# A gated cross-attention block with eight experts on one core: the first expert's tokens are taken unweighted and its sum weighted apart, and the router's exponential moves to GpSimd

## The reference

```python
router_logits = x @ gate_w.T                      # 448 x 8
probs = softmax(router_logits)
topw, sel = top_k(probs, 2)
topw = topw / sum(topw)
combine = sum(one_hot(sel, 8) * topw[..., None], axis=1)
gate, up = split(x @ gate_up_w[e].T)              # 512 columns each, for every expert e
hact = up * gelu(gate)
expert_out = hact @ down_w[e].T
out = sum_e expert_out[e] * combine[:, e]
```

## Time and profile before

| | us |
|---|---|
| median of 3 runs | 279.33 (279.15 to 280.34) |
| the profiled execution | 282.56 |
| its span, first to last instruction | 280.8 |
| PE busy | 268.3 (96%) |
| DVE busy | 217.1 (77%) |
| ACT busy | 178.9 (64%) |
| POOL busy | 125.7 (45%) |

### The profile page before, as it was taken

The page is one execution under the profiler, slowest core; times in us unless marked ns, Lnnn a source line. Parts: engine busy times, 40 slices in busy tenths (PEclk is TensorE's granted clock), DMA queues, the critical chain, the costliest instruction groups (busy, mean ns, idle before and its releaser), DMA issues.

```text
span 280.8 us, 8075 instructions
## 1 busy us (share of the span) xinstructions
PE 268.3 (96%) x2807; PEld 220.5 (79%) x2807; DVE 217.1 (77%) x460; ACT 178.9 (64%) x369; POOL 125.7 (45%) x148
## 2 busy tenths in 40 slices
PE   7989899999999999999999999988989999999994
PEld 3466678888888888887988887876888788989962
DVE  4679778878887889788878897886566988888771
ACT  2546677677776777678668765564718877776500
POOL 3588852574466456455456210123520855554200
PEclk9999999999999999999999999997999999999999
DMA  7389972991992992794595399200000000000001
GB/s 249 100 203 206 192 188 57 244 234 39 234 234 71 247 223 79 179 239 133 156 234 159 79 219 292 80 0 2 2 2 1 0 4 0 0 1 0 0 0 33
DMA packets 10821, 32.40 MB, mean 115 GB/s; under 512 B 2688, under 2 KB 3200, under 8 KB 10784
## 3 DMA queue, kind: packets, MB, share of 16 engines
q1 hardware_dynamic: 10368, 31.80, 44.7%
q10 hardware_dynamic: 432, 0.33, 0.4%
HBM read 13.26 MB, written 0.23 MB: 48 GB/s over the span
## 4 chain that ended last, share of the span: by engine, by line
PE 79%; ACT 6%; DVE 6%; DMA 3%; issue 2%; POOL 1%; SPq 1%; DVEq 0%; ACTq 0%
PE max_ps L1065 15%; PE o_ps L1086 14%; PE score_ps L1045 14%; PE misc_ps L1024 8%; PE misc_ps L1017 4%; DMA kx<-k_high 3%; PE score_ps L1281 3%; ACT probs L560 3%; PE score_ps L1282 2%; PE score_ps L1283 2%; PE o_ps L1383 2%; PE misc_ps L1125 2%; DVE part_max L746 2%; PE o_ps L1281 2%; PE score_ps L1009 2%
## 5 line engine op out<-in xcount | busy, mean ns | idle before, releaser
L746 DVE TENSOR_REDUCE part_max<-max_ps 112x1 f32<-112x512 f32 (+1 forms) x192 | 117.6, 666 | 28.1 <-PE max_ps L1065 26.4
L560 ACT ACTIVATE probs<-score_ps 128x448 f32<-128x448 f32 x188 | 88.2, 548 | 13.8 <-PE score_ps L1045 13.5
L1065 PE MATMUL max_ps<-kx,qx 96*112 96x512 f32 (+1 forms) x192 | 79.7, 421 | 3.4 <-DMA kx<-k_high 1.5
L1045 PEld LDWEIGHTS score_ps<-qx,kx 104*128 104x128 f32 x376 | 64.4, 190 | 8.1 <-issue 0.7
L1045 PE MATMUL score_ps<-qx,kx 104*128 104x224 f32 x376 | 67.8, 278 | 0.0
L1086 PE MATMUL o_ps<-probs,v_sb 128*32 128x112 f32 (+1 forms) x1536 | 46.2, 265 | 1.1 <-ACT probs L560 0.6
L1086 PEld LDWEIGHTS o_ps<-probs,v_sb 128*32 128x32 f32 (+1 forms) x1536 | 38.4, 111 | 7.5 <-ACT probs L560 6.1
L1065 PEld LDWEIGHTS max_ps<-kx,qx 96*112 96x112 f32 x192 | 33.6, 176 | 9.9 <-issue 4.6
L554 ACT ACTIVATE v_sb<-misc_ps 128x512 f32<-128x512 f32 x24 | 14.4, 602 | 29.4 <-PE misc_ps L1024 29.4
L381 POOL TENSOR_TENSOR k_low<-k_full,k_high 128x512 fp32r<-128x512 f32 (+1 forms) x21 | 26.3, 1256 | 13.7 <-ACT k_full L542 13.4
L417 POOL CAST ctx_parts<-ctx_sb 128x512 fp32r<-128x512 f32 (+1 forms) x18 | 10.8, 602 | 41.5 <-PE misc_ps L1017 26.7
(11 more groups left out here) (192 smaller groups left out, 387.4 us busy)
## 6 DMA issues: line engine op xcount, KB each, us to landing
kx<-k_high SPq DMA_DIRECT2D x60, 187.5 KB, 4.6
kx<-k_low SPq DMA_DIRECT2D x30, 187.5 KB, 4.5
gu_sb<-in_guT SPq DMA_DIRECT2D x8, 512.0 KB, 5.2
ctx_sb<-in_ctxT SPq DMA_DIRECT2D x6, 494.0 KB, 5.5
ctx_sb<-in_ctxT SPq DMA_DIRECT2D x8, 256.0 KB, 2.8
dn_sb<-in_dnT SPq DMA_DIRECT2D x8, 256.0 KB, 5.7
ctx_sb<-in_ctxT SPq DMA_DIRECT2D x1, 750.0 KB, 6.3
kx<-k_high SPq DMA_DIRECT2D x4, 123.5 KB, 2.3
```

The source lines that it names most:

```text
L560: nc.scalar.activation(probs[:, (KT * h + t) % 8, :], bank[:, 0:SC // 2], ACT.Exp, scale=SCALE).then_inc(exp_done, 1)
L746: nc.vector.reduce_max(part_max[:, p, c:c + 1], max_ps[0:PC, bank, 0:size], AX.X).then_inc(max_taken, turns)
L1045: last = nc.tensor.matmul(bank[0:m, GC * g:GC * g + GC], kx[0:KR, 2 * par + h, g, 128 * t:128 * t + m], qx[0:KR, par, 2 * h + g, :], start ...
L1065: nc.tensor.matmul(max_ps[0:PC, bank, 0:size], qx[0:MR, par, 2 * h + p // 2, PC * (p % 2):PC * (p % 2) + PC], kx[0:MR, slot, p // 2, start ...
```

## The change

- **First expert.** Its ups take `x_high` and `x_low`, the unweighted tokens. `spread_first`, the three steps that made its weighted tokens and the matmul by zeros are gone. Its downs are a sum of their own in `o_ps`. `spread_weight(0, 0)` lays its weights over a bank; DVE copies them to SBUF (`weight_first`) inside expert 0, ahead of `x_expert_full` for expert 1. After expert 0, DVE waits for its downs and multiplies the sum by the weights (`y_first`). The sum of experts 1 to 7 starts afresh in `o_ps` once that is done, and at the end DVE adds `y_first` to it in place of ACT's copy.
- **Exponential.** POOL raises a tile of e's (`euler`, 112 x 32, filled earlier) to the power of the logits with `ALU.pow`, once the last row's logits have their maximum subtracted. ACT's exponential is gone, and its gelu of one column stands behind the copies of the first 336 tokens, ahead of those of the last 112.
- **Tokens.** ACT makes `x_high` first; DVE takes the low part from the PSUM bank, not from `xnT`; ACT copies `xnT` after that. The router's products on PE, which read `xnT`, come later.
- **Order on PE.** Three gate blocks of 336 tokens ahead of the last out projection; `route` for three rows behind it; the gates' last 112 tokens partly ahead of `route` for the last row, and block 1 of expert 1 among the blocks done in two pieces. Then the first ups, among them the transposition of the weights after the third.
- **Order on DVE.** `less_max` for three rows stands inside the last row's layer norm, before `compare`.
- **Order on POOL.** The selecting matrices do not wait for expert 0's tokens, and there is one more.

The diff, cut to its core:

```diff
@@ gpsimd
+            serial(nc.gpsimd.memset(euler[:, :, :], EULER))
...
+            pool.wait_ge(router_step, LOGITS_MADE)
+            nc.gpsimd.tensor_tensor(pr[:, :, :], euler[:, :, :], logits[:, :, :], ALU.pow).then_inc(logits_exp, 1)
             pool.wait_ge(rows_ready, 1)
             weights_rest(GATE, 2, 0, 5)
             def expert(i, par):
                 e = batch(i, par)
-                pool.wait_ge(xe_ready, e + 1)
+                if e:
+                    pool.wait_ge(xe_ready, e)
                 select(e + 1, 1 - par)
...
+            select(0, 0)
@@ scalar
             act.wait_ge(xT_done, 2)
+            nc.scalar.activation(x_high[:, 0:OWN], early_xT_ps[:, 0:OWN], ACT.Copy).then_inc(xT_saved, 1)
+            act.wait_ge(x_split, 1)
             nc.scalar.activation(xnT[:, 0:OWN], early_xT_ps[:, 0:OWN], ACT.Copy).then_inc(xT_saved, 1)
-            nc.scalar.activation(x_high[:, 0:OWN], early_xT_ps[:, 0:OWN], ACT.Copy).then_inc(xT_saved, 1)
...
+            nc.scalar.activation(scratch[:, :], tanh_g[:, 0:1], ACT.Gelu)
             act.wait_ge(ffn_loaded, 16 * (1 + 2 * E))
             act.wait_ge(xT_done, 3)
+            nc.scalar.activation(x_high[:, OWN:TOK], xT_ps[:, OWN:TOK], ACT.Copy).then_inc(xT_saved, 1)
+            act.wait_ge(x_split, 2)
             nc.scalar.activation(xnT[:, OWN:TOK], xT_ps[:, OWN:TOK], ACT.Copy).then_inc(xT_saved, 1)
-            nc.scalar.activation(x_high[:, OWN:TOK], xT_ps[:, OWN:TOK], ACT.Copy).then_inc(xT_saved, 1)
-            act.wait_ge(router_step, LOGITS_MADE)
-            nc.scalar.activation(pr[:, :, :], logits[:, :, :], ACT.Exp).then_inc(logits_exp, 1)
-            nc.scalar.activation(scratch[:, :], tanh_g[:, 0:1], ACT.Gelu)
...
-            act.wait_ge(down_done, E * FT)
-            nc.scalar.activation(yT, o_ps[:, 0:TOK], ACT.Copy).then_inc(y_saved, 1)
@@ vector
-            nc.vector.memset(zeros.bitcast(f32), 0.0).then_inc(zeros_ready, 1)
...
-                nc.vector.tensor_tensor(x_low[:, first:end], xnT[:, first:end], x_high[:, first:end].bitcast(f32),
+                nc.vector.tensor_tensor(x_low[:, first:end], bank[:, first:end], x_high[:, first:end].bitcast(f32),
                                         ALU.subtract).then_inc(x_split, 1)
-            less_max(0, NR - 1)
-            attended(3, NR - 1, NR, lambda: compare(0, NR - 1))
+            def first_logits():
+                less_max(0, NR - 1)
+                compare(0, NR - 1)
+
+            attended(3, NR - 1, NR, first_logits)
...
-            x_expert_full(0, 0)
-            x_expert_copy(0, 0)
-            x_expert_rest(0, 0)
+            def weigh_first():
+                dve.wait_ge(first_weighed, 1)
+                dve.wait_ge(down_done, FT)
+                nc.vector.tensor_tensor(y_first, o_ps[:, 0:TOK], weight_first, ALU.mult).then_inc(first_weighed, 1)
...
                 product(3)
+                if first:
+                    dve.wait_ge(bc_done, 1)
+                    nc.vector.tensor_copy(weight_first, max_ps[:, 0, 0:TOK]).then_inc(first_weighed, 1)
                 x_expert_full(e + 1, 1 - par)
...
+            dve.wait_ge(xT_saved, 5)
+            expert(0, 0, first=True)
+            weigh_first()
+            expert(0, 1)
...
+            dve.wait_ge(down_done, E * FT)
+            nc.vector.tensor_tensor(yT, o_ps[:, 0:TOK], y_first, ALU.add).then_inc(y_saved, 1)
@@ tensor
+            gate_part(0, 0, 0, OWN)
+            gate_part(0, 1, 0, OWN)
+            gate_part(1, 1, 0, OWN)
             project_out(NR - 1, FIRST_NORM + NU)
+            pe.wait_ge(xT_saved, 3)
+            route(0, NR - 1)
+            gate_part(0, 2, 0, OWN)
             pe.wait_ge(x1_ready, NR)
             gate_part(1, 0, 0, OWN)
+            keep_warm(2, o_ps)
             transpose_tokens(NR - 1, NR, NR)
+            gate_part(0, FT - 1, 0, OWN)
+            pe.wait_ge(x_split, 2)
+            gate_part(0, 0, OWN, TOK).then_inc(gate_done, 1)
+            pe.wait_ge(xT_saved, 5)
             route(NR - 1, NR)
-            pe.wait_ge(x_split, 2)
-            for j in range(FT):
+            for j in range(1, FT):
                 gate_part(0, j, OWN, TOK).then_inc(gate_done, 1)
-            gate_part(1, 0, OWN, TOK).then_inc(gate_done, 1)
-            pe.wait_ge(router_step, LOGITS_MADE)
-            gate(1, 1, first_banks[1])
-            spread_first()
+            for j in range(2):
+                gate_part(1, j, OWN, TOK).then_inc(gate_done, 1)
...
+                if first:
+                    pe.wait_ge(weights_low, made)
+                    pe.wait_ge(gelu_ready, FT - 1)
+                    up(e, par, 0, (x_high, x_low))
+                    pe.wait_ge(gelu_ready, FT + 1)
+                    up(e, par, 1, (x_high, x_low))
+                    pe.wait_ge(router_step, LOGITS_MADE)
+                    up(e, par, 2, (x_high, x_low))
+                    transpose_weights()
+                    up(e, par, 3, (x_high, x_low))
...
                 next_gate(0)
                 next_gate(1)
+                if first:
+                    pe.wait_ge(gelu_ready, FT + 2)
+                    spread_weight(0, 0)
+                elif fresh:
+                    pe.wait_ge(first_weighed, 2)
                 spread_weight(e + 1, 1 - par)
                 down(0)
```

## The result

The changed kernel is slower: median 283.79 us over 6 executions (282.79 to 285.16) against 279.65 over 6 of the kernel before, a ratio of 1.0139 with an interval from 1.0106 to 1.0171. By the ratio that is +3.9 us (4.1 by the two medians), where 281.7 was forecast, +2.4 on the 279.33 known then. The direction and the place were right, the size was not, and 283.79 lies above the range of 278.9 to 283.5. The ratios in this document leave out executions in a slower state: of all the runs only two of e7's twelve (284.09 and 284.89), which its median still counts.

What follows compares the result with a forecast made beforehand. TensorE was taken to bound the kernel from expert 1's first up on. That up moved by +2.2 + 0.55 - 0.4 = +2.35, the last add +0.07: +2.4 on 279.33, median 281.7 us, range 278.9 to 283.5.

Steps and rivals of the forecast that it cites:

- The point on which it turned: ACT's queue: the copy of `combT` stands ahead of three weight copies and all of expert 0, so delaying it delays those.
- Part 1: Up to the last row's logits: they come 0.9 us later, at 212.7 instead of 211.74.
- Part 2: Gelus and first ups come earlier: first gelu at 212.0 instead of 213.50, first up at 215.0 instead of 217.2.
- Part 3: POOL's power takes 5.0 us, `comb_ready` at 219.2 instead of 214.34, weights' transposition +3.0; net +2.2 after relief.
- the same pace as before: From expert 1's first up, forecast at 228.5, PE goes on at an unchanged pace.
- The relief of 1.1: DVE's `rest`s in expert 0 overlap less with POOL's work: 0.7 us back at the first two, 0.4 at the next two.
- the copy of 0.55: DVE's copy of the spread weights from PSUM inside expert 0 delays the chain to expert 1's ups by 0.55 us.
- part 4: Weighting apart in expert 0: +0.55 for the weight copy, -0.4 at the next `rest`s; `weigh_first`, 0.6, covered.
- (a): Rival: TensorE's clock also falls after PE's wait and slows expert 1's ups, priced at 1.5 us; 283.2 us, chance 0.12.
- (b): Rival: POOL's power takes below about 2.6 us and hides; net within 0.3 us of nothing, 279.3 us, chance 0.18.
- (c): Rival: power cheap, and the earlier gelus and ups carry 1.4 us to the end; 277.9 us, chance 0.13.

Runs made afterwards that it cites:

- e7: The changed kernel with the power over 4 columns instead of 32, same result, and POOL held until the combine weights are ready; 279.91 us, ratio 0.9995.
- e6: The changed kernel with POOL held as in e2 and two of ACT's weight copies put ahead of its `combT` copy; 282.79 us, ratio 1.0110.
- e2: The changed kernel with POOL waiting for `comb_ready` before its low part of expert 2's gate weights; 283.44 us, ratio 1.0154.
- e3: The kernel before with only the exponential moved to POOL's power and the gelu table loaded early; 285.28 us, ratio 1.0205.
- e5: The changed kernel with 11 idle-filling matmuls ahead of PE's wait for `comb_ready`; 283.48 us, ratio 1.0140.
- e1: The changed kernel with the exponential back on ACT, behind the copy of `xnT`, and the gelu table loaded behind it; 283.97 us, ratio 1.0158.
- e4: The changed kernel with the power over 8 columns instead of 32, the other exponentials left out, so its result is not the reference's; 279.71 us, ratio 0.9994.
- e8: e7 with e6's order on ACT; 279.37 us, ratio 0.9980, its profiled execution with the clock at 0.50 in the gates and first ups.
- e8_again: The kernel of e8 run once more; 279.31 us, ratio 1.0005.
- e10: The kernel before with four idle-filling matmuls in PE's wait for DVE before the last attention unit; 278.94 us, ratio 0.9974.

## Why the prediction was right or wrong

**The point on which it turned: right.** ACT's queue carries the delay of `combT` to all behind it (+4.3, +4.2, +4.2 in three successive columns), and e6 moved the first `hact_copy` by 1.04 by taking two copies out of it. How far that reaches is another matter: 0.26 of it was left at the end.

**Part 1: right.** The last logits came 10.42 after the landmark (210.66 + 0.17), forecast 10.5; `xn` and the low part at their forecast distances within 0.1.

**Part 2: right.** First gelu at 9.95 after the landmark (forecast 9.8), first ups ready to run before the weights, PE at its wait 0.1 from the forecast distance.

**Part 3: the sum failed here.** Three pieces of it.
The power: 5.48 where I took 5.0, though my own upper bound, the step from three columns to four carried on to 32, was 5.5 and hit it. +0.5. By the rule of the Trainium skill ("GPSIMD Engine Reference", Performance versus the Vector engine) it would have been some 0.4, an estimate from its 2.6 cycles per element; it speaks of adds, and the trace, with 5.48, does not bear it out for a power.
What stands behind the power on its own engine: I wrote that the power "holds up the low part of expert 2's gate weights" and asked only who reads that low part. I did not ask whom its start would hold up, and so the sum has no term for it. It starts at the power's end, in the microsecond in which DVE has the router's steps: +0.6 (e2 against the changed kernel). The Trainium skill ("SBUF — State Buffer", SBUF: two separate sides) says that a GpSimd instruction that reads SBUF and a VectorE instruction with two inputs in SBUF exclude each other, and that the one that starts first keeps the other out for its whole length. By that rule L932 waits for the subtraction's end, and the trace agrees (217.61 and 217.65), but it would also have to wait behind the power itself, and there the trace disagrees: L911 reads two SBUF inputs at 211.12, inside the power of 210.90 to 216.38, and takes its usual 0.22.
The step from the power's end to DVE's next instruction: 0.49 where I allowed 0.1: +0.4. It belongs to the changed kernel, not to the power (0.11 behind the same power in e3), and its cause stays open.
Together +1.5, less 0.1 because the power started that much sooner than forecast. The trace shows 1.3 at the weights' transposition (18.40 against a forecast 17.1) and 1.4 at expert 1's first up (27.76 against 26.4). From there on I wrote "the same pace as before" and added 0.07 for the last add; the trace gives back 0.6 instead, which I had not foreseen. Without that luck the miss would be larger: +3.2 at the end of the profiled span, +3.7 at expert 1's first up.

**The relief of 1.1 and the copy of 0.55, part 4: right in sum.** From the first `hact_copy` to expert 1's first up it is 6.38 in the changed kernel and 6.88 before, -0.50; forecast -0.55. In its parts: the first two `rest`s end 2.69 after the start of the first `hact_copy` instead of 3.28 (0.6 of relief for a forecast 0.7), the next two take 1.14 instead of 1.60 (0.5 for 0.4), and the copy, 0.61 long, delays the chain by 0.53. `weigh_first` was covered, as said. e6 shows that the relief is a matter of phase: start the `rest`s 1 us earlier and it is gone.

**The rivals.** (a), the clock: it fell after the stall as its rival said, and in the profiled execution cost nothing (e5). As a price it is real elsewhere: 1.4 and 1.1 us in e1, 1.6 in e3, 1.2 in e4, 2.0 in e8. The measured median lies 3.9 above, the traces explain 3.2; what is left fits the executions' clocks (spans of 281.1 at a mean of 0.992, 282.0 to 282.2 at 0.986 and 0.987, 283.4 at 0.981), but e5, with the stall's low stretch removed, was not faster by its ratio (1.0140). With six and four executions this stays open. (b), the cheap power: its condition did not hold, its price did: e4 and e7 are level with before, as worked out. (c), the lead that carries: it needed the transposition at 214.9, which is 12.7 after the landmark. In e4 and e7, with a short power and the gelus 1.3 us early, it stands at 14.75, and expert 1's first up in e7 at 24.11 against 24.02 before: the lead did not reach it. PE's nine ups and ACT's order stood between, and taking ACT's order away (e8_again) gave half a microsecond in the trace.

**The range** failed with the sum: 1.4 us of missing terms on a forecast of 2.4, and its high end left out the case of a longest power together with a clock that falls.

## What to carry to other kernels

A slow instruction put on an idle engine is not free on that account: what counts is who waits for it, and what stands behind it in its own queue and starts the moment it ends. Price it by rows of the same operation, fit a line through them, and then shrink its operand before moving it: here four columns carried the same information as thirty-two, and that was worth 3.6 us.
A wait of a microsecond or more on TensorE can cost more than itself, because the clock may fall behind it (it fell behind a wait of 1.8 us in e1 and e4, not in e7); look at which work would then run at the lower clock, and fill the wait if that work is on the path. It paid in e10, and not in e5, where PE had slack behind the wait.
When one execution of each kernel is profiled, compare where its clock was low before comparing its time: e1 and e3 would otherwise have been read as prices of the order on the engines.

## What the runs showed of the hardware that I had not expected

- GpSimd's power costs 0.16 us per column of 112 partitions, evenly from 1 to 32 columns (0.60, 0.87, 1.03, 1.69, 5.48 us for 1, 3, 4, 8 and 32), while a multiply of 112 columns takes 0.42.
- A GpSimd subtraction of 512 columns in SBUF stretches even a VectorE instruction of 32 columns to its own end: 0.78 us instead of 0.19. Two VectorE subtractions of 448 columns in SBUF took 2.69 us beside it and 1.14 without.
- In the changed kernel and its variants with powers of 8 and 32 columns VectorE went on 0.49 us after the power's recorded end; after powers of 1, 3 and 4 columns, and after one of 32 columns in e3, it was 0.1. So it does not follow the power's length. What it follows stays open.
- The granted clock stood at 0.50 after a wait of PE of 0.95 us for a gelu (e1) and after one of 1.8 us for VectorE (e1, e4; not e7). After one of 1.33 us ahead of the last attention unit it did so in six of eleven profiles; with that wait filled, in neither of two, and no execution of e10 had a low mean clock.
